# Transposed weights of layer 1 in four transfers, another order in the first and last steps, and attention sums from the split weights

## The reference

```
h = relu(layernorm(x))
q, k, v = h Wq' + bq, h Wk' + bk, h Wv' + bv
w = adj * exp(q k');  w = w / sum(w, axis=2)
x = x + w v
h = relu(layernorm(x))
agg = (adj h) / max(sum(adj, -1), 1e-6)
x = x + relu([h, agg] W')
```

## Time and profile before

| | us |
|---|---|
| median of 3 runs | 1939.62 |
| lowest, highest | 1936.89, 1942.41 |
| profiled execution, its own time | 1942.48 |
| its span | 1940.4 |
| busy: PE, weight loads, VectorE, ScalarE, GpSimd | 1892.7, 1576.8, 1579.6, 862.4, 1103.0 |
| DMA engines busy, HBM traffic | 57.2%, 191 GB/s |

### The profile page before, as it was taken

How to read it: one execution, slowest core, us unless ns; L and a number is a source line. 1 busy time by engine, 2 the same in 40 slices (tenths; PEclk the granted TensorE clock), 3 DMA queues, 4 the chain that set the end, 5 groups by cost and what they waited for, 6 DMA issues and landing times.

```text
span 1940.4 us, 29261 instructions
## 1 busy us (share of the span) xinstructions
PE 1892.7 (98%) x8956; PEld 1576.8 (81%) x8956; DVE 1579.6 (81%) x2649; ACT 862.4 (44%) x1453; POOL 1103.0 (57%) x1066
## 2 busy tenths in 40 slices
PE   8899999999999999999999999999999999999997
PEld 5778888888888888888788888888888888887885
DVE  6887888888788888888878888887888878888776
ACT  4344444444444445443445443444444454434442
POOL 4665565565565565655655655655655656546552
PEclk9999999999999999999999999999999999999999
DMA  6456656566656566555566555566555665555632
GB/s 222 148 189 212 210 181 196 188 203 207 210 178 190 198 205 204 192 198 173 189 208 219 188 194 184 191 211 211 179 191 194 204 203 194 197 173 184 211 125 87
DMA packets 190881, 370.69 MB, mean 191 GB/s; under 512 B 17936, under 2 KB 115216, under 8 KB 182672
## 3 DMA queue, kind: packets, MB, share of 16 engines
q1 hardware_dynamic: 190864, 370.48, 57.2%
HBM read 266.60 MB, written 103.81 MB: 191 GB/s over the span
## 4 chain that ended last, share of the span: by engine, by line
PE 49%; DVE 19%; DMA 17%; issue 8%; SPq 4%; POOL 2%; ACT 1%; DVEq 1%; POOLq 0%; ACTq 0%
PE bank L518 16%; PE bank L520 16%; PE bank L519 16%; DMA turned_store<-blocks 8%; DMA n_l<-t_store 8%; DVE y L1223 3%; SPq L263 3%; DVE x L1235 3%; DVE stats L1091 2%; DVE x L1227 2%; DVE g_full L1213 2%; DVE deg L1112 1%; DVE mean_sum L1096 1%; DVE blocks L1073 1%; DVE sums L1252 1%
## 5 line engine op out<-in xcount | busy, mean ns | idle before, releaser
L403 POOL TENSOR_TENSOR hT_l<-turned,hT_h 128x512 fp32r<-128x512 f32 x122 | 181.9, 1517 | 264.0 <-ACT hT_h L824 263.9
L242 POOL TENSOR_TENSOR w_l<-w,w_h 128x512 fp32r<-128x512 f32 x62 | 80.3, 1295 | 307.5 <-ACT w_h L857 307.5
L1073 DVE STREAM_TRANSPOSE blocks<-h 128x512 f32<-128x512 f32 x252 | 163.3, 685 | 110.3 <-DMA turned_store<-blocks 110.3
L518 PE MATMUL bank<-hT_h,n_h 128*128 128x512 f32 x512 | 200.9, 392 | 3.9 <-DVE hT_l L1164 2.8
L519 PE MATMUL bank<-hT_l,n_h 128*128 128x512 f32 x512 | 200.2, 391 | 0.0
L520 PE MATMUL bank<-hT_h,n_l 128*128 128x512 f32 x512 | 200.2, 391 | 0.0
L518 PE MATMUL bank<-wv_h,hT_h 128*128 128x512 f32 x512 | 199.6, 390 | 0.0
L519 PE MATMUL bank<-wv_l,hT_h 128*128 128x512 f32 x512 | 199.5, 390 | 0.0
L520 PE MATMUL bank<-wv_h,hT_l 128*128 128x512 f32 x512 | 199.3, 389 | 0.0
L399 POOL TENSOR_TENSOR xb<-x_in,bv_b 128x512 f32<-128x512 f32 x128 | 165.9, 1301 | 43.5 <-DVE x L1235 39.3
L843 ACT ACTIVATE kz_h<-bank,kp_bias 128x512 fp32r<-128x512 f32 x128 | 83.6, 675 | 207.5 <-PE bank L520 207.5
(11 more groups left out here) (152 smaller groups left out, 5394.9 us busy)
## 6 DMA issues: line engine op xcount, KB each, us to landing
turned_store<-blocks SPq DMA_DIRECT2D x126, 512.0 KB, 4.5
turned<-turned_store SPq DMA_DIRECT2D x504, 128.0 KB, 2.9
x_in<-x SPq DMA_DIRECT2D x32, 1024.0 KB, 5.3
n_h<-t_store SPq DMA_DIRECT2D x31, 1024.0 KB, 6.3
n_l<-t_store SPq DMA_DIRECT2D x31, 1024.0 KB, 8.3
out<-x SPq DMA_DIRECT2D x124, 256.0 KB, 2.0
n_h<-n_store SPq DMA_DIRECT2D x60, 512.0 KB, 4.6
n_l<-n_store SPq DMA_DIRECT2D x60, 512.0 KB, 5.9
```

The source lines that it names most:

```text
L242: engine.tensor_tensor(w_l[:, g], w[:, g], w_h[:, g].bitcast(F32), ALU.subtract).then_inc(w_split, 1)
L403: pool.tensor_tensor(by_blocks(hT_l, t), turned_tile(t), by_blocks(hT_h, t).bitcast(F32), ALU.subtract).then_inc(hT_split, 1)
L518: pe.matmul(dst, lh, rh, start=first, stop=False, skip_group_check=more)
L1073: nc.vector.transpose(blocks[:, :, :, t % NT, :].rearrange("p j c b -> p c j b"), h[:, t, :].rearrange("p (c j b) -> p c j b", c=DT, b=Q)) ...
```

## The change

The key sums come straight from the split weights. For each of the 4 tiles of queries and each of its 2 key blocks the block's 128 columns of `w_h`, and then of `w_l`, are the stationary operand, and two columns of ones the moving one: sixteen matmuls in place of two. The result has the queries on the partitions, so that the mask and the reduction are gone, and with them the additions, `sum_h` and `sum_l`. `load_t` is cut into halves (T1, T2), each a high and a low transfer of 512 KB, and each half stands between the store and the load of a half of the turned g. The third product waits for the first half, the fourth for the second. In the first step w1_t is loaded before the next x, N is stored after T2 and the adjacency, the transposed h parts and the stores of T1 and T2 are interleaved otherwise, and the mixes have other places on ScalarE and GpSimd; T4 is made in the first step, not in the second. In the last two steps the results, S2, S4, z and the degrees change places.

```diff
             def split_w(engine, i, g):
...
-            engine.wait_ge(w_split, G * i + g + 1)
-            engine.tensor_tensor(w[:, g, 0, :], w[:, g, 0, :], w[:, g, 1, :], ALU.add).then_inc(w_summed, 1)
...
-            def move_g(j):
+            def move_g(j, with_t=True):
                 for g in range(G):
                     store_blocks(1, g, g_turned, T * j + NT * (g + 1), g_stored)
+                    if with_t:
+                        if g == 0:
+                            sp.wait_ge(kp_psum, DT * (j + 2))
+                        load_t(g)
                     sp.wait_ge(g_stored[g], 16 * (j + 1))
                     load_turned(1, g, g_moved)
...
-            def load_t(i):
-                sp.wait_ge(kp_psum, DT * (i + 1))
-                sp.dma_start(n_h[:, :, :].bitcast(F32), t_d[0]).then_inc(t_loaded, 16)
-                sp.dma_start(n_l[:, :, :].bitcast(F32), t_d[1]).then_inc(t_loaded, 16)
+            def load_t(k):
+                half = slice(2 * k, 2 * k + 2)
+                sp.dma_start(n_h[:, half, :].bitcast(F32), t_d[0, :, half, :]).then_inc(t_loaded, 16)
+                sp.dma_start(n_l[:, half, :].bitcast(F32), t_d[1, :, half, :]).then_inc(t_loaded, 16)
...
+            sp.wait_ge(setup_psum, DT)
+            sp.wait_ge(parts_done, 2 * DT + 1)
+            sp.dma_start(x1[:, :, :], w1_t[0:dim].rearrange("(t p) o -> p t o", p=P)).then_inc(wh_loaded, 16)
             sp.wait_ge(xb_done, T)
             load_x(1)
-            sp.wait_ge(setup_psum, DT + 2)
-            sp.dma_start(x1[:, :, :], w1_t[0:dim].rearrange("(t p) o -> p t o", p=P)).then_inc(wh_loaded, 16)
-            sp.wait_ge(n_split, DT)
-            sp.dma_start(n_d[0], n_h[:, :, :].bitcast(F32)).then_inc(n_stored, 16)
-            sp.dma_start(n_d[1], n_l[:, :, :].bitcast(F32)).then_inc(n_stored, 16)
...
             def first_step():
-                move_h(1)
+                store_blocks(0, 0, h_turned, NT, h_stored)
                 store_t(0, T1)
+                sp.wait_ge(h_stored[0], 16)
+                load_turned(0, 0, h_moved)
+                store_blocks(0, 1, h_turned, T, h_stored)
+                sp.wait_ge(h_stored[1], 16)
+                load_turned(0, 1, h_moved)
+                store_t(1, T2)
                 load_adj(0)
-                store_t(1, T2)
+                sp.wait_ge(n_split, DT)
+                sp.dma_start(n_d[0], n_h[:, :, :].bitcast(F32)).then_inc(n_stored, 16)
+                sp.dma_start(n_d[1], n_l[:, :, :].bitcast(F32)).then_inc(n_stored, 16)
...
             def sum_weights(i, dst):
-                pe.wait_ge(sum_split, i + 1)
-                every, all_ones = bank[dst][:, :], ones[:, 0:1].to_broadcast([P, P])
-                pe.matmul(every, all_ones, sum_h[:, :, :].rearrange("p g n -> p (g n)"), start=True, stop=False)
-                mm = pe.matmul(every, all_ones, sum_l[:, :, :].rearrange("p g n -> p (g n)"), start=False, stop=True)
+                pe.wait_ge(w_split, G * (i + 1))
+                for t in range(T):
+                    g, qt = divmod(t, NT)
+                    cols = slice(qt * P, (qt + 1) * P)
+                    for c in range(NT):
+                        pe.matmul(bank[dst][:, 2 * t:2 * t + 2], w_h[:, g, c, cols], ones[:, :], start=(c == 0), stop=False)
+                        mm = pe.matmul(bank[dst][:, 2 * t:2 * t + 2], w_l[:, g, c, cols], ones[:, :], start=False,
+                                       stop=(c == NT - 1))
                 mm.then_inc(sum_psum, 1)
...
                 pe.wait_ge(part_split, 7 * j + S1)
-                pe.wait_ge(t_loaded, 32 * i)
+                pe.wait_ge(t_loaded, 64 * j + 32)
...
                 pe.wait_ge(part_split, 7 * j + S2)
+                pe.wait_ge(t_loaded, 64 * (j + 1))
...
             def final_step(i):   # ScalarE
...
                 high_at(j)
+                copy_p0(j, 0)
+                copy_p0(j, 1)
                 act.wait_ge(combined, 4 * j + 3)
                 high_part(j, S2)
+                high_z(j, 0)
+                high_z(j, 1)
                 high_part(j, A22)
-                copy_p0(j, 0)
-                copy_p0(j, 1)
                 act.wait_ge(combined, 4 * j + 4)
                 high_part(j, S4)
-                high_z(j, 0)
-                high_z(j, 1)
...
             def sum_inverses(i, sum_bank):   # VectorE
                 dve.wait_ge(sum_psum, i + 1)
+                every = bank[sum_bank][:, 0:2 * T].rearrange("p (t k) -> p t k", k=2)
+                nc.vector.reciprocal(sum_inv[:, :], every[:, :, 0]).then_inc(sum_inv_done, 1)
...
             def final_step(i):   # VectorE; combine_s4 stood at the end of last_step
                 j = i - 1
+                sum_z(j, 0)
+                sum_z(j, 1)
+                low_z(j, 0)
+                low_z(j, 1)
+                combine_s4(j)
                 degrees(j)
-                sum_z(j, 0)
-                low_z(j, 0)
-                sum_z(j, 1)
-                low_z(j, 1)
```

More of the change, by code:

```diff
@@ L119, in gnn_layers @@
         adjT = sb("adjT", [P, T, nodes])
-        with nc.sbuf_tensor("z_full", [P, ROUNDS, dim], F32) as z_full:
-            z_sum = (z_full[:, 0], z_full[:, 1])
-        sum_h, sum_l = sb("sum_h", [P, G, nodes], F32R), sb("sum_l", [P, G, nodes], F32R)
+        z_full = sb("z_full", [P, ROUNDS, dim])
+        z_sum = (z_full[:, 0], z_full[:, 1])
         w = sb("w", [P, G, NT, nodes])
@@ L417, in mix @@
                 pool.tensor_tensor(dst, a, b, ALU.subtract).then_inc(mixed, 1)
-            def low_sum(i):
-                pool.wait_ge(sum_high, i + 1)
-                pool.tensor_tensor(sum_l[:, :, :], w[:, :, 0, :], sum_h[:, :, :].bitcast(F32),
-                                   ALU.subtract).then_inc(sum_split, 1)
             def low_at(i):
@@ L448, in first_step @@
                 pool.wait_ge(wh_loaded, 16)
+                pool.wait_ge(setup_psum, DT + 2)
                 mix(wb_parts, wh_raw[1], wh_raw[0])
-                for g in range(G):
-                    scale_and_shift(0, 1, g)
                 low_mix(T3)
-                pool.wait_ge(mixed, 1)
+                scale_and_shift(0, 1, 0)
+                scale_and_shift(0, 1, 1)
                 mix(wh_raw[0], wh_raw[0], wz_raw[0])
@@ L504, in final_step @@
                 low_part(j, A12)
-                for m in (S1, S3, S2, A22):
+                for m in (S1, S3, S2):
                     low_part(j, m)
                 low_at(j)
+                low_part(j, A22)
                 low_part(j, S4)
@@ L857, in high_w @@
                 nc.scalar.activation(w_h[:, g], w[:, g], ACT.Copy).then_inc(w_high, 1)
-            def high_sum(i):
-                act.wait_ge(w_summed, G * (i + 1))
-                nc.scalar.activation(sum_h[:, :, :], w[:, :, 0, :], ACT.Copy).then_inc(sum_high, 1)
             def high_part(j, m):
@@ L890, in first_step @@
                 high_kp(0, 0)
+                high(mix_h[B22][:, :, :], mix_raw[B22], wh_loaded, 16, b22_high)
                 high_kp(0, 1)
-                high_kp(0, 2)
                 act.wait_ge(mixed, 1)
                 high_mix(T3)
+                high_kp(0, 2)
                 high_kp(0, 3)
                 act.wait_ge(key_bias_done, T)
-                relu_norm(0, x_in, 1, 0)
-                relu_norm(0, x_in, 1, 1)
-                relu_norm(0, x_in, 1, 2)
-                relu_norm(0, x_in, 1, 3)
-                high(mix_h[B22][:, :, :], mix_raw[B22], wh_loaded, 16, b22_high)
+                for t in range(T):
+                    relu_norm(0, x_in, 1, t)
                 high_v(0, 0)
@@ L910, in first_step @@
                 high_v(0, 1)
-                high_sum(0)
-                high_v(0, 2)
-                high_v(0, 3)
-                act.wait_ge(v_psum, T)
-                for t in range(NT):
-                    high_hT(1, t)
                 act.wait_ge(mixed, 3)
@@ L919, in first_step @@
                 high_mix(T2)
-                for t in range(NT, T):
+                high_v(0, 2)
+                high_v(0, 3)
+                act.wait_ge(mixed, 4)
+                high_mix(T4)
+                act.wait_ge(v_psum, T)
+                for t in range(T):
                     high_hT(1, t)
@@ L1241, in layer1_stats, with sum_inverses @@
                 tile_stats(1, src, t)
-            def sum_inverses(i, sum_bank, key_biases):
-                dve.wait_ge(key_bias_done, key_biases)
+            def sum_inverses(i, sum_bank):
                 dve.wait_ge(sum_psum, i + 1)
-                own = h[:, 0, :].rearrange("p (t n) -> p t n", t=T)
-                every = bank[sum_bank][:, :].rearrange("p (t n) -> p t n", t=T)
-                mask = diagonal[:, :].rearrange("p (a n) -> p a n", a=1).to_broadcast([P, T, P])
-                nc.vector.tensor_tensor(own.bitcast(I32), every.bitcast(I32), mask,
-                                        ALU.bitwise_and).then_inc(sum_taken, 1)
-                dve.wait_ge(sum_taken, 2 * i + 1)
```

(5 more changed lines are left out.)

50 lines of the change are left out of this document (15 added, 35 removed).

## The result

| | before | after |
|---|---|---|
| median, us | 1938.26 (4 runs) | 1981.89 (4 runs, 1974.83 to 1985.2) |
| ratio, 95% interval | | 1.0219 [1.0183, 1.0254] |
| profiled execution: own time, span | 1942.48, 1940.4 | 1980.08, 1978.3 |

The kernel became 2.2% slower. 1940 was forecast, with 1957 as the upper end of the range. The likeliest case failed, and what came is the rival that was called *g late* and given 1975 us.

The account below looks back on a forecast made before the run. PE, 98% busy, was taken as the bound. Sums +42.3, t -26.3, first steps -10 and final step -5.6 gave +0.4 us on the 1939.6 us median: 1940 us, with an 8-in-10 range of 1919 to 1957.

Parts of the forecast that it names:

- The likeliest case: Whole kernel: small matmuls at weight-load pace, t's wait hidden, first and last steps better; 1940 us, chance 0.70.
- g late: Rival, loop: t's halves delay the turned g by 2.4 us each, the fourth product waits; 1975 us, chance 0.08.
- Key sums, +42.3: Every step's sums: sixteen small matmuls at 0.111 us replace two of 0.23, +1.32 us a step, 32 times.
- covered loads: Rival, key sums: small matmuls' weight loads run ahead, 0.014 to 0.05 us each; 1899 to 1908 us, chance 0.12.
- t in four transfers, -26.3: Loop: t's halves, issued earlier, arrive before their products; stalls fall to 1 us in all, saving 26.3 us.
- So each half delays g by about 0.5 us, and the second by 1.2 us with the first's: Loop queue: 2.4 us per half at 438 GB/s, about 2 us of it fitting into idle DMA time before g's load.
- nothing on PE: Loop, fourth product: 0.9 us of slack and up to 2.7 us of lead outweigh g's 1.2 us delay.
- The slack of 3.6 us: Loop: g's delay makes the fourth product wait only from 0.9 + 2.7 = 3.6 us on.
- The lead of 2.7 us: Between steps: VectorE's tail 1.4 us shorter, PE's 1.3 longer, so x1, norms and turned g come up to 2.7 earlier.
- First steps, -10: First step and into the second: new order brings hT, keys and sums earlier, shortening waits and half clock; 10 us saved.
- the ends don't move: Rival, first and last steps: the new order only passes waits on, the -15.6 is absent; 1956 us, chance 0.10.
- Final step, -5.6: Last step: z's sum and low parts go earlier, cutting the 5.3 us z wait and half clock; 5.6 us saved.

Follow-up runs that it names:

- e3: The kernel before with only the new sums (sixteen small matmuls, old sum operations removed), t and all orders as before: 1953.02 us, ratio 1.006.
- e4: The kernel before with t in four transfers in front of g's loads and the new final order, but old sums and first step: 2006.73 us, ratio 1.0325.
- e1: The changed kernel with T2's transfers moved behind the load of the second half of the turned g: 1950.95 us, ratio 1.0055 to the kernel before.
- b3: The kernel before with only t changed: two halves behind both loads of g, each waited for on its own semaphore: 1920.3 us, ratio 0.9853.
- e5: e1 with the first step, set-up transfers and mixes in their order of before: 1949.64 us, ratio 1.0054 to the kernel before.
- e7: e1 with GpSimd's last two first-step mixes waiting until both halves of the first w are split: 1949.83 us, ratio 1.0055 to the kernel before.
- b4: b3 with the change's new final-step order added: 1914.2 us, ratio 0.9866 to the kernel before.
- e6: e1 with each step's sixteen small matmuls made twice, back to back: 2080.76 us, ratio 1.0726 to the kernel before.
- e8: e1 with a second set of sixteen small matmuls behind the second av product, in steps 1 to 30: 2004.2 us, ratio 1.0287 to the kernel before.

## Why the prediction was wrong, point by point

- **Key sums, +42.3: right.** Measured +43.2 (clean step +1.35 us against +1.32). The row of the f32 loads gave the right price, 0.111 us; *covered loads* is refuted.
- **t in four transfers, -26.3: wrong, and this is the miss.** Measured +3.2 in the loop, 29.5 us away. The step that failed is "So each half delays g by about 0.5 us, and the second by 1.2 us with the first's", which rested on a standstill of the DMA engines of about 2 us, and ended in "nothing on PE". What the runs show in its place: the two halves together let the second half of g land 3.5 us later (median, after against e3), 2.1 us of it by T2 and the rest by T1; the stalls behind it are the 30.5 us. Two errors are in the step. The 438 GB/s came from a single microsecond; over the stretch that matters the nearly full engines move 249 to 338. And the standstill was an effect of the old order: with T1 and T2 in the queue it is filled before the load comes. Against the kernel before the issue of the load is only 0.7 us later after the sums, within what was predicted; the landing is 2.3 us later. What was to be watched was the landing.
- **The slack of 3.6 us: too high.** From e3's landing to the point where the fourth product becomes late it is 2.4 us. The lead of 2.7 us was there for the queue (e3), but with the new sums S2's low part is ready 0.8 us ahead of the product even where g lands early, so 0.9 and 2.7 don't add up there. e4 shows what the lead is worth: without it the waits more than double. The rival *g late* named the mechanism and came within 7 us of the time, but by luck: its delay (4.8 us against 3.5) and its slack (3.6 against 2.4) were too high by about the same.
- **What was not seen: the gains overlap.** The lead of the new sums removes the wait for t by itself (e3). The transfers' new place, even without T2's delay, adds nothing to the new sums (e1 1.0055, e3 1.006). Put where it was, split in halves, t gives its 22 us without them (b3: stalls 4.9 against 27.3).
- **First steps, -10: too high.** Measured -3.6, and -6.7 without T2's delay (e1). The order itself is worth nothing (e5). The chain was followed with the durations of before, in which GpSimd was idle beside nearly all of these operations; in the new order both run, and VectorE's 3.2 us become 9.8. The first sums, expected earlier, come 2.7 us later and run behind a wait of 3.02 us at half clock: from 62.56 to the matmul of 512 columns behind them at 65.99 they take 3.43 us, twice the price. Taking the collision away moves the wait on (e7), as the rival *the ends don't move* has it.
- **Final step, -5.6: right.** Measured -4.9, alone -4.5 (b4 against b3). Timeline of PE after, the two waits that were one of 5.28 us:

```profile
1956.76 0.47 PE L508 MATMUL bank<-kz_h,at_h 128*128 128x512 f32 x1 [0.43 <-DVE kz_l L1053]
...
1959.50 0.50 PE L508 MATMUL bank<-mix_h,hT_h 128*128 128x512 f32 x1 [1.13 <-ACT g_full L869]
```

The clock is granted at 1.00 there, and the half level of the earlier trace rows is gone.
- **The signs.** Sixteen in 1.8 us, the step of 59.3, no wait for t, no late issue of g, and the short wait for z all came as said. The second sums, at 127 instead of 121, did not, and the waits for g that were to be the sign of failure came. Five signs held beside a forecast that was 42 us off: none of them looked at the landing of g.

What stays open: why the landing of g differs by up to 3.4 us from step to step of the same kernel, which decides whether a step waits. The residue of 4.5 us in e1 lies for the most part in five steps of the same kind, with landings at 35.0 to 36.4.

## What to carry to other kernels

A standstill of the DMA engines in a trace belongs to the order that left it; before a transfer is put into it, count what the new order already queues there, and price a transfer by its row from issue to landing, not by the best microsecond of bandwidth. Where two edits remove waits, ask whether it is the same wait: here the cheaper of the two alone (halves with semaphores of their own, behind the urgent load) gave 1.5% (b3), and the other alone cost 0.6% (e3). A matmul with few columns isn't cheap if it brings weights of its own: here one of 2 columns cost half of one of 512.

## What the runs showed of the hardware

- A matmul of 2 columns behind 128 columns of its own fp32r weights costs 0.11 us at full clock and 0.21 at half, against 0.23 for 512 columns.
- Behind 32 of them in a row the granted clock fell to its half level in nearly every step of e6 (0.56 from 1023.20 to 1026.60), though PE counts as busy and nothing waits; in e8, with the same 32 in two sets of 16 and 512-column matmuls between, it stayed at 1.00.
- VectorE's operations with two inputs in memory become up to 4.4 times as long beside GpSimd's (1.30 to 5.66 us for two), and GpSimd's x goes from 2.39 us (in e7) to 2.85. The Trainium skill (SBUF — State Buffer, section SBUF: two separate sides) has these two share a pair of ports that one instruction locks for its whole length. The rows agree: each of VectorE's two takes 2.8 us, the length of one of GpSimd's (2.85 and 2.74).
